# Windowed attention's projections as plain f32 products with double-buffered weights and in-block set-up, and full attention's values in halves

## The reference

```python
x = x + full_attention(layernorm(x))      # 16 heads of 8, low-rank terms in the projections
x = x + channel_mix(layernorm(x))
x = x + full_attention(layernorm(x))      # causal
x = x + channel_mix(layernorm(x))
x = x + rg_lru(layernorm(x))
x = x + window(layernorm(x))
x = x + full_attention(layernorm(x))      # plain
x = x + window(layernorm(x))

def window(x):                            # 6 layers, 16 heads of 64, window 32
    for i in range(6):
        h = shift_tokens(x)               # channels 64.. come from the token before
        q, k, v = split(h @ Wqkv[i], 3)
        q, k = l2norm(q) * qs[i], l2norm(k) * ks[i]
        q = q * cos * scale + rotate_half(q) * sin * scale
        k = k * cos / scale + rotate_half(k) * sin / scale
        # a block of 32 queries sees its own 32 keys and the 32 before
        x = local_attention(q, k, v, 8.0) @ Wo[i] + x
        n = layernorm(shift_tokens(x)) * g[i] + bln[i]
        a, gate = split(n @ W1[i] + b1[i], 2)        # 341 columns each
        x = (a * gelu(gate)) @ W2[i] + b2[i] + x
    return x
```

## Time and profile before

| | |
|---|---|
| median of 3 runs | 6007.92 us (6006.31 to 6008.05) |
| profiled execution | 6016.27 us |
| span of its records | 6014.3 us |
| PE busy | 5498.8 us, 91% |
| DVE, ACT, POOL busy | 4315.4, 4082.8 and 2765.6 us |
| DMA | 87.16 MB, mean 14 GB/s |

### The profile page before, as it was taken

How to read it: one execution, slowest core, us unless ns; L and a number is a source line. 1 busy time by engine, 2 the same in 40 slices (tenths; PEclk the granted TensorE clock), 3 DMA queues, 4 the chain that set the end, 5 groups by cost and what they waited for, 6 DMA issues and landing times. The chain is left out here.

```text
span 6014.3 us, 154805 instructions
## 1 busy us (share of the span) xinstructions
PE 5498.8 (91%) x57658; PEld 3896.3 (65%) x57658; DVE 4315.4 (72%) x6698; ACT 4082.8 (68%) x7766; POOL 2765.6 (46%) x2459
## 2 busy tenths in 40 slices
PE   8887996799999999999997888799999999999997
PEld 3223332677777777777776322677777778777775
DVE  7875645677777777777775886777777777777774
ACT  5774654577777777777774577577777777777774
POOL 1101100565656665556663110666556566555662
PEclk8997997899999999999999899899999999999998
DMA  0000000100000000000000000100000000000000
GB/s 12 1 1 5 2 1 9 32 18 15 18 16 15 22 15 21 14 19 16 17 20 10 4 1 1 35 16 17 18 14 19 17 16 22 14 18 16 16 20 16
DMA packets 128105, 87.16 MB, mean 14 GB/s; under 512 B 32596, under 2 KB 121200, under 8 KB 127320
## 3 DMA queue, kind: packets, MB, share of 16 engines
q1 hardware_dynamic: 127320, 76.74, 4.5%
HBM read 68.96 MB, written 1.05 MB: 12 GB/s over the span
## 5 line engine op out<-in xcount | busy, mean ns | idle before, releaser
L1742 POOL TENSOR_TENSOR cross<-raw,tab_b 128x512 f32<-128x512 f32 x768 | 999.2, 1325 | 291.7 <-ACT raw L1612 288.8
L732 DVE TENSOR_REDUCE arena<-PS 128x1 f32<-128x512 f32 (+3 forms) x1408 | 837.6, 648 | 252.5 <-PE PS L550 162.1
L1748 POOL CAST kT_b<-kT 128x512 bf16<-128x512 f32 x384 | 300.0, 781 | 1317.5 <-ACT kT L1666 1317.5
L683 ACT ACTIVATE arena<-PS 128x1024 f32<-128x1024 f32 (+1 forms) x704 | 656.4, 968 | 324.0 <-PE PS L573 238.5
L1841 DVE TENSOR_TENSOR oT<-PS,rec_den 128x288 f32<-128x288 f32 (+1 forms) x768 | 326.4, 425 | 637.2 <-ACT rec_den L1646 637.2
L1812 DVE TENSOR_TENSOR rot<-PS,tab_a 128x512 f32<-128x512 f32 x768 | 522.5, 686 | 233.0 <-PE PS L1491 142.7
L1460 PE MATMUL PS<-qT,kT 64*128 64x96 f32 x8448 | 659.3, 286 | 0.0
L1612 ACT COPY raw<-PS 128x512 f32<-128x512 f32 x768 | 448.0, 591 | 287.7 <-PE PS L1491 247.3
L1638 ACT ACTIVATE PT<-PS 128x576 f32<-128x576 f32 (+1 forms) x768 | 468.9, 611 | 254.3 <-PE PS L1460 243.3
L1828 DVE TENSOR_TENSOR rot<-rot,cross 128x1024 f32<-128x1024 f32 x384 | 611.7, 1593 | 13.3 <-POOL cross L1742 11.3
L550 PE MATMUL PS<-k_parts,q_parts 32*128 32x512 f32 (+3 forms) x1408 | 505.4, 509 | 92.7 <-DVE arena L732 78.3
(11 more groups left out here) (255 smaller groups left out, 12972.2 us busy)
## 6 DMA issues: line engine op xcount, KB each, us to landing
w_qk<-in_w_pairs SPq DMA_DIRECT2D x196, 128.0 KB, 2.1
w_v<-in_w_pairs SPq DMA_DIRECT2D x100, 128.0 KB, 2.2
w_o<-in_w_out_pairs SPq DMA_DIRECT2D x192, 64.0 KB, 1.8
xs<-staged SPq DMA_DIRECT2D x24, 254.0 KB
w<-in_L_ffn_W SPq DMA_DIRECT2D x12, 341.0 KB
q_parts<-max_rows SPq DMA_DIRECT2D x192, 2.0 KB
raw<-in_c_E SPq DMA_DIRECT2D x2, 896.0 KB, 4.5
w<-in_L_ffn_W SPq DMA_DIRECT2D x24, 64.0 KB
```

The costliest lines, as they stand in the source:

```text
L683: nc.scalar.activation(PT[u % 4].rearrange("p (a n) -> p a n", a=2)[:, :, first_q:512], PS[:, 2 * (u % 2):2 * (u % 2) + 2, first_q:512], A ...
L732: nc.vector.tensor_reduce(maxima[:, 2 * m + h, qt, kh:kh + 1], bank[:, 0:keys_of(qt, kh)], AX.X, ALU.max).then_inc(bank_free, 1)
L1742: nc.gpsimd.tensor_tensor(dst[:, :, :, o:o + 32], src[:, :, :, other:other + 32], tab[:, :, o:o + 32].unsqueeze(2).broadcast_to([128, 8, 2 ...
```

## The change

In **window_layers** Q, V, G and A become one plain f32 matmul each, from `x_turned` (one buffer per batch), `nT` and the weights as loaded. All splits and low parts go, on GpSimd, ScalarE and VectorE. `w_qk`, `w_v` and `w_o` have two buffers, each with its semaphore; a reload of a buffer waits for the fill that last read it (Q3 or V5). The set-up is part of the block: SP issues first qk weights, bases, V weights, 8 rows of scales, E, mask, then the second buffers; each engine prepares batch 0 (`bring_in(0)`) and, after position (0, 0, 0), batch 1 (`second_batch`). GpSimd zeroes only pads and makes R, E and mask in bf16, behind waits for them; the first copy of V waits for these constants. The running `x` is `x_run`, written by the normalising; `x_tok` stays as it is, so the copy to `x_keep` goes.

In **full attention** `values` comes in halves of 256 query columns: `values(t - 1, 0)` in slot 1 of step t, `values(t - 2, 1)` in slot 0 of the step after. `PT` has six buffers and the exponentials wait for the values of two steps back. In the causal one each half has one empty product ahead, and a half that is masked out is left out.

```diff
-    x_keep = sb("x_keep", [128, TILES, C])
-    PRODUCTS = ((0, 0), (0, 1), (1, 0))
+    x_run = sb("x_run", [128, TILES, C])
...
-        PT = [cut(2 * 512) for m in range(4)]
+        PT = [cut(2 * 512) for m in range(6)]
...
-                def values(t):
+                def values(t, part):
...
+                    lo, hi = max(first_query(hf, kt), 256 * part), 256 * part + 256
+                    if part == 0:
+                        pe.wait_ge(exp_done, 2 * t + 2)
+                        if kt == 0:
+                            need(pe, o_ev, 2 * i + hf)
+                        if t % STEPS == 0:
+                            pe.wait_ge(vb_ready, i + 1)
...
+                    if lo < hi:
+                        for hh in range(4):
+                            last = nc.tensor.matmul(PS[32 * hh:32 * hh + 32, 6, lo:hi], VB[i % 2][:, kt, hh, :],
+                                                    PT[(2 * t + hh // 2) % 6][:, 512 * (hh % 2) + lo:512 * (hh % 2) + hi],
+                                                    start=kt == 0 and part == 0, stop=t == last_step(2 * i + hf), tile_position=(0, 32 * hh),
+                                                    skip_group_check=True)
+                    if part == 1:
+                        last.then_inc(pv_done, 1)
...
-                            values(t - 1)
+                            values(t - 1, 0)
+                        if slot == 0 and 1 < t <= ALL + 1:
+                            values(t - 2, 1)
...
-                    need(act, pv_done, t - 1)
+                    need(act, pv_done, t - 2)
...
-        x_parts = [[own(f"x_{name}{b}", [128, XW], F32R) for name in ("high", "low")] for b in range(B)]
-        w_qk, w_v, w_o = own("w_qk", [128, 256]), own("w_v", [128, 2, 128]), [own(f"w_o{m}", [128, C]) for m in range(2)]
-        wqk_parts = [own(f"w_qk_{name}", [128, 256], F32R) for name in ("high", "low")]
-        wv_parts = [own(f"w_v_{name}", [128, 256], F32R) for name in ("high", "low")]
+        x_turned = [own(f"x_turned{b}", [128, XW]) for b in range(B)]
+        w_qk, w_v, w_o = ([own(f"{name}{m}", shape) for m in range(2)] for name, shape in (("w_qk", [128, 256]), ("w_v", [128, 2, 128]), ("w_o", [128, C])))
...
-        def layers(eng, position):
+        def layers(eng, position, second_batch):
             for b, p in PLACES:
                 position(0, b, p)
+                if (b, p) == (0, 0):
+                    second_batch()
...
-                        need_apart(sp, wqk_split, it * 2 + 4)
+                        need_apart(sp, full, fill(l, b, p, "Q3") + 1)
...
-                            need(sp, wv_split, ff_index(l, b) * 8 + (8 + 2 * j + 4))
+                            need(sp, full, fill(l, b, p, "V5") + 1)
...
                 qk_weights(0, 0)
+                sp.dma_start(base_a[:, :, :], I["c_rot_a"].rearrange("p (t n) -> p t n", t=BT)).then_inc(bases_in, 16)
+                sp.dma_start(base_b[:, :, :], I["c_rot_b"].rearrange("p (t n) -> p t n", t=BT)).then_inc(bases_in, 16)
+                v_weights(0, 0)
                 scale_rows(0)
-                v_weights(0, 0)
-                sp.wait_ge(wqk_split, 2)
+                sp.dma_start(st_E, I["c_E"]).then_inc(loaded, 16)
+                sp.dma_start(st_mask, I["c_blocks"]).then_inc(loaded, 16)
                 qk_weights(0, 1)
-                sp.wait_ge(wv_split, 2)
                 v_weights(0, 1)
                 ff_weights(0)
...
+                def second_batch():
+                    turn_in(1)
+                    pe.wait_ge(zeroed, ZEROED)
+                    pe.wait_ge(consts_made, 4)
...
-                        need(pe, wqk_split, item(l, b, p) * 2 + 2)
+                        if isinstance(l, int) and l == 0 and p == 0:
+                            pe.wait_ge(set_in, 2 * b + 2)
+                        need(pe, wqk_in[p % 2], l * 128 + (64 * b + 16 * (p // 2) + 16))
...
-                        for n, (m, w) in enumerate(PRODUCTS):
-                            last = nc.tensor.matmul(bank[:, 256 * j:256 * j + 256], x_parts[b][m][:, PAD + 128 * t:PAD + 128 * t + 128], wqk_parts[w][:, :],
-                                                    start=n == 0, stop=n == 2)
+                        last = nc.tensor.matmul(bank[:, 256 * j:256 * j + 256], x_turned[b][:, PAD + 128 * t:PAD + 128 * t + 128], w_qk[p % 2][:, :],
+                                                start=True, stop=True)
...
-                                need(pe, wv_split, phi * 8 + (8 + 2 * j + 2))
+                                need(pe, wv_in[j % 2], phi * 32 + (32 + 16 * (j // 2) + 16))
...
-                                need(pe, nl_done, phi * 2 + (k + 1))
-                                need(pe, w1_split, (l + b) * 2)
+                                taken(pe, l, b, 3, f"N{k}")
+                                need(pe, ff_in, (l + b) * 96)
...
-                            nc.scalar.activation(nT[:, 512 * f:512 * f + 512], bank, ACT.Identity, scale=ff_cols[:, 6:7], bias=ff_cols[:, 7:8])
-                            nc.scalar.activation(n_parts[0][:, 512 * f:512 * f + 512], bank, ACT.Identity, scale=ff_cols[:, 6:7],
+                            nc.scalar.activation(nT[:, 512 * f:512 * f + 512], bank, ACT.Identity, scale=ff_cols[:, 6:7],
...
-                def split(parts, w, loaded, count, done, number):
-
-                    need(pool, loaded, count)
-                    nc.gpsimd.tensor_tensor(parts[0][:, :].rearrange("p (i n) -> p i n", i=2), w.rearrange("p (i n) -> p i n", i=2),
-                                            ones[:, :].unsqueeze(1).broadcast_to([128, 2, 128]), ALU.mult).then_inc(done, 1)
-                    need(pool, done, number * 2 + 1)
-                    nc.gpsimd.tensor_tensor(parts[1][:, :], w, parts[0][:, :], ALU.subtract).then_inc(done, 1)
...
-                        need(pool, full, fill(l, b, p, "Q3") + 1)
-                        split_qk(it + 1)
...
+                pool.wait_ge(loaded, 32)
+                nc.gpsimd.tensor_copy(E[:, :, :].rearrange("p e n -> p (e n)"), st_E).then_inc(consts_made, 1)
+                nc.gpsimd.tensor_copy(block_mask[:, :, :].rearrange("p c n -> p (c n)"), st_mask).then_inc(consts_made, 1)
+                pool.wait_ge(bases_in, 32)
+                layers(pool, position, lambda: None)
...
+                def bring_in(b):
+                    for t in range(BT * b, BT * b + BT):
+                        nc.vector.bn_stats(stats[:, t, :], x_tok[:, t, :]).then_inc(set_stat, 1)
+                    for t in range(BT * b, BT * b + BT):
+                        dve.wait_ge(set_stat, 2 * BT * b + t % BT + 1)
+                        nc.vector.bn_aggr(moments[:, t, :], stats[:, t, :]).then_inc(set_stat, 1)
+                    dve.wait_ge(set_rs, b + 1)
+                    for t in range(BT * b, BT * b + BT):
+                        nc.vector.tensor_scalar(x_run[:, t, :], x_tok[:, t, :], moments[:, t, 0:1], rstd[:, t:t + 1],
+                                                ALU.subtract, ALU.mult).then_inc(set_normed, 1)
+
+                def second_batch():
+                    bring_in(1)
+                    dve.wait_ge(zeroed, ZEROED)
+
+                bring_in(0)
+                dve.wait_ge(bases_in, 32)
+                layers(dve, position, second_batch)
```

More of the change, by code:

```diff
@@ L1599, in position @@
                             scores(l, b, p, r, s + 1)
+                            if isinstance(l, int) and l == 0 and (b, p) == (0, 1) and s == 0:
+                                pe.wait_ge(set_in, 4)
                             values(r, s, (p + 7) % 8)
                         late(l, b, p, s + 2)
-                layers(pe, position)
+                turn_in(0)
+                layers(pe, position, second_batch)
             @block.scalar
@@ L1607, in _ @@
                 load_ln_exp()
+                def bring_in(b):
+                    tiles = slice(BT * b, BT * b + BT)
+                    act.wait_ge(set_stat, 2 * BT * (b + 1))
+                    nc.scalar.activation(rstd[:, tiles], moments[:, tiles, 1], ACT.Ln, bias=eps_ap).then_inc(set_lnv, 1)
+                    act.wait_ge(set_lnv, b + 1)
+                    nc.scalar.activation(rstd[:, tiles], rstd[:, tiles], ACT.Exp, scale=-0.5).then_inc(set_rs, 1)
+                    act.wait_ge(zeroed, ZEROED if b else X_ZEROED)
+                    for k in range(2 * b, 2 * b + 2):
+                        own_token, next_token = shifted_columns(x_turned[b], k % 2)
+                        act.wait_ge(set_turned, k + 1)
+                        nc.scalar.copy(own_token, PS[0:64, 4 + k, :])
+                        nc.scalar.copy(next_token, PS[64:128, 4 + k, 0:512 - k % 2]).then_inc(set_in, 1)
+                def second_batch():
+                    bring_in(1)
                 def raw_copy(l, b, p, i):
```

194 lines of the change are left out of this document (56 added, 138 removed).

## The result

The changed kernel takes 6077.94 us (median of 4 runs, 6066.34 to 6090.40) beside 6007.11 for the kernel before: a ratio of 1.0117, 95% interval 1.0102 to 1.0132. Measured a second time it gave 6082.84, ratio 1.0122 (1.0104 to 1.0140). It is slower by 71 us where 48 were forecast; 6055 with a range of 5955 to 6140 holds it.

A forecast was written before the change was run, and what follows sets the result against it. TensorE was taken to set the pace of the window layers. Products +137, set-up −35 and attention −55 made +47 on 6016.27, so 6063 us, or 6055 on the median's scale; range 5955 to 6140.

The forecast's parts named there:

- terms (1) to (3): Window layers, TensorE: plain products cost +241 us (queries, keys, values) and +61 (feed-forward), saved group starts −97; gross +205.
- Term (3): Window layers, TensorE: the 0.10 us that starting an fp32r group costs goes away, −97 us.
- term (1): Window layers, TensorE: queries, keys and values at 0.45 us a plain product against 0.357 split, +241 us.
- term (4): Window layers, TensorE: idle spots (4.7 us a half layer, 113 in all) take in 60% of the added work, −68 us.
- the work taken off other engines … is costed at nothing: Window layers: dropping GpSimd's splits, a ScalarE pass and VectorE's low parts saves nothing, since it lay beside TensorE's work.
- rival D: Window layers: with splits gone, chains beside TensorE shorten and all 4.7 us of waiting could go; +2, 6010 us; chance 0.16.
- Rival B: Window layers: idle spots move instead of filling, so they absorb nothing; +115, 6123 us; chance 0.17.
- Each position would wait for a transfer of about 2 us: Window weight loads: two buffers keep the DMA hidden, some 40 us ahead; without that cover, every position waits about 2 us.
- The sines: Window set-up: GpSimd's table of sines should be free about 3 us after the cosine products begin, as before.
- bound by TensorE, +15: Causal full attention: bound by TensorE, so halves (+9) and later accumulator copies (+6) cost 15 us together.
- steps with a fill … should gain more: Plain full attentions: fill steps of 3.3 us gain more than plain ones; −4.4 us per 16 steps, −70 for two attentions.
- Rival A: Full attention: halving lets fill steps run at VectorE's speed, under 2.8 us; attentions fall from 390 toward 320; 5985; chance 0.14.

The follow-up runs named there:

- copy moved: Changed kernel with split products put back, plus the copy of a finished half moved behind its step's first exponential on ScalarE in full attention: 5911.03 us, ratio 0.9843.

## Why the prediction held, and where it was off

The forecast was +137 for the products, −35 for the set-up, −55 for attention, +47 in all. The runs give +146, −34 and −45, so +67, beside a measured +71.

**The product, terms (1) to (3).** The path was right: two records in place of three starts, each about twice as long per column. The gross cost was 205 in the forecast and is 9.06 us a half layer of TensorE's busy time (182.50 − 173.44), 217 in all. But it came out so near by two errors that offset each other. Term (3) let the start of a group, 0.10 us, go with fp32r. It doesn't go for queries, keys and values: their plain products have the same start (above). And term (1) took 0.45 us a product where the rows have 0.432. Queries, keys and values cost 7.3 us a half layer, 175 in all, for the 241 − 82 = 159 of (1) with its share of (3); G and A cost 1.7, 41 in all, for 61 − 15 = 46. Of the signs, position 2, expected to stay nearly as it was, grew by 0.9 us, and positions 5 and 6 by 1.4 (from first Q to first Q). The Trainium skill (FP8 and Floating Point Precision, TensorE Precision Notes) counts four passes for true FP32. At 0.119 us a pass that makes an estimate of 0.476 us, which the trace doesn't bear out: 0.432 for a product, and 0.48 only where two products share a group's start.

**Idle time, term (4).** The 60% nearly stood: 3.1 of the 4.7 us went (65%). Of gross 9.1 us a half layer 6.0 show. But I gave one cause for it, and there are two. With the splits kept, 7.4 of the 9.1 show, so 1.7 us, 40 in all and not 68, are taken in by waits as such; another 1.4, 34 in all, come from splits and low parts that are gone. The step "the work taken off other engines … is costed at nothing" is the one that failed, by some 34 us; rival D named it, but not all idle time goes. The sum 217 − 40 − 34 = 143 stands beside the 146 of the runs. That two causes make 74 us where 68 stood for one is luck. Rival B (nothing absorbed) is out: position 3 took its products in.

**The cover of the weight loads.** "Each position would wait for a transfer of about 2 us" was wrong in kind. Without the second buffer one position in eight waits, for 8.1 us, and the clock makes it dearer: 248 us. What must be costed is what stands ahead of the load, on SP and among the transfers, not the load alone.

**Set-up.** 24 us sooner was right to a tenth. The second batch costs 5.6 us (8.2 − 2.6) where 6 was taken. The sines are the miss: GpSimd has their table 6.4 us after the cosine products begin (1055.50 − 1049.05), not 3, and 2.7 us of that are exposed. By the trace that is 15.6 a call; the runs have 17.

**Attention.** Plain steps of 2.46 us for the 2.5 forecast. The wrong step is the causal one: "bound by TensorE, +15". It became shorter, 342.7 to 329.6 us. In it VectorE was waiting as well, and for TensorE's products:

```profile
L732 DVE TENSOR_REDUCE arena<-PS 128x1 f32<-128x512 f32 (+3 forms) x382 | 193.9, 551 | 127.2 <-PE PS L560 87.5 <-PE PS L550 38.6
```

```profile
L736 DVE TENSOR_REDUCE arena<-PS 128x1 f32<-128x512 f32 (+3 forms) x382 | 194.8, 552 | 114.8 <-PE PS L559 80.0 <-PE PS L549 32.1
```

The first row is of the kernel before, the second of the changed one: 12.4 us of VectorE's waiting are gone, 13.1 the stretch. A 94% busy TensorE was read as a bound, though each engine was waiting for the other in turn. The stretch also spent less time at the lower clock, 75.1 us for 88.7; how much of the 13 us is owed to that no run separates.

And the plain ones gained less than 70: some 32 with 45 in all and 13 in the causal one, and some 21 by the traces (384.4 and 385.0 us beside the 395.0 and 395.6 without a stray stretch). The step that failed is "steps with a fill … should gain more". These are the medians of the third attention, by place in the round of 16 steps (start to start of four reductions, us):

```
                                       before            after             copy moved
nine plain steps, each                 2.70              2.39 to 2.61      2.39 to 2.65
five steps with fills, each            3.29 to 3.52      2.86 to 3.50      2.86 to 3.49
two steps at the group's end, both     8.4               10.6              8.9
all 16                                 49.4              48.3              46.7
```

The forecast had −4.4 for the 16; −1.1 was measured. What most steps gained, the end of a group took back: TensorE's maxima wait 12.2 us in the third attention for ScalarE's fill copies, before 3.5, and six of the eight ends bring 3.4 to 6.8 us at the lower clock. Rival A's sign, fill steps under 2.8 us, did not come either; its 320 us fell short at that place: 385.0 us, and 374.1 with the copy moved.

**The sum.** The forecast lies 24 us low: the products were 9 us dearer, attention 10 poorer, the set-up 1, and 4 are the scatter between the runs' sum and the whole. The likeliest case came, with D's mechanism inside it, and with the help of errors that offset each other in the gross cost, in the idle time and, in attention, between the causal one (28 us better than forecast) and the two plain ones (some 38 poorer).

## What to carry to other kernels

Price a change of precision by the records: take the spacing of equal matmuls at the same width, and count starts for both kinds. Here an f32 product of 256 columns is 0.432 us and three fp32r ones 0.357, each with 0.10 more for a group; the splits that this asks for cost GpSimd 713 us of work (w_qk's and w_v's alone) and the program some 30. When a cover is costed, look at what the issuing engine waits for and sends ahead of the load. When two executions of the same code differ, compare the granted clock stage by stage first. An engine that is 94% busy is not yet the bound: ask what the second engine's waits are for.

## What the runs showed that was not expected

A two-column instruction of GpSimd lasts 0.20 or 1.17 us, depending on what VectorE is doing. The Trainium skill (SBUF — State Buffer, SBUF: two separate sides) says that a VectorE operation with two SBUF inputs and a GpSimd operation lock the port pair that they share for a whole instruction; these rows agree, the short one ending with VectorE's. The prediction took the 1.6 us of a split for its own length and found the rule to overstate. But 0.73 us is what a split takes when VectorE does not stand in its way, and the 0.43 us that VectorE lost in the earlier trace rows fits within that.

In attention, a group's end with a wait of 1.7 us on TensorE was followed by a granted clock of 0.50 (1.2 GHz); with 0.76 us in its place the clock stayed at 1.00. Like the wait of 8.1 us above, it costs more than its length. And an unchanged attention varied by 13 us (395.0 to 407.7) with the time that it spent at the lower level.
